# An adaLN-style layer on one core: GpSimd's low parts of x1 and x2 held back, the last tile's h turned earlier, sign's first slice in two transfers, 17 warm-ups for 19

## The reference

```python
base = einsum('btd,od->bto', x, W)
logits = einsum('btd,ed->bte', x, Wr) + 5.0 * one_hot(itok)[:, None, :]
topw, topi = top_k(logits, 2); weights = softmax(topw)
gates = sum(one_hot(topi, 8) * weights[..., None], axis=-2)
h = einsum('btd,erd->bter', x, A)
cond = base + 2.0 * einsum('bter,bte,eor->bto', h, gates, B)
out = x + einsum('bsi,io->bso', cond, sign) * softplus(scale)
```

## Time and profile before

| | us |
|---|---|
| median of 3 runs | 163.86 (163.75 to 163.94) |
| the profiled execution | 163.53 |
| its span (first to last instruction in the profile) | 161.3 |
| PE busy | 157.4 (98% of the span) |
| DVE busy | 110.0 (68%) |
| ACT busy | 63.6 (39%) |
| POOL busy | 52.2 (32%) |

### The profile page before, as it was taken

How to read it: one execution, slowest core, us unless ns; L and a number is a source line. 1 busy time by engine, 2 the same in 40 slices (tenths; PEclk the granted TensorE clock), 3 DMA queues, 4 the chain that set the end, 5 groups by cost and what they waited for, 6 DMA issues and landing times.

```text
span 161.3 us, 3653 instructions
## 1 busy us (share of the span) xinstructions
PE 157.4 (98%) x1046; PEld 151.8 (94%) x1046; DVE 110.0 (68%) x451; ACT 63.6 (39%) x178; POOL 52.2 (32%) x50
## 2 busy tenths in 40 slices
PE   8999999999999999999999999999999999999993
PEld 5887889899999999999999999999999999999992
DVE  5999999566666667666656666676666666666641
ACT  3645622244433334234344444433444343334432
POOL 2975554333330323333333333223132333333000
PEclk9999999999999999999999999999999999999999
DMA  5995332335545545344454545555555362223333
GB/s 178 376 150 131 107 107 74 89 76 150 147 142 148 142 104 180 106 135 123 126 142 136 139 142 146 143 146 145 144 146 145 86 189 81 62 62 87 130 130 130
DMA packets 45867, 21.47 MB, mean 133 GB/s; under 512 B 23680, under 2 KB 40864, under 8 KB 45856
## 3 DMA queue, kind: packets, MB, share of 16 engines
q1 hardware_dynamic: 30232, 13.58, 31.0%
q10 hardware_dynamic: 15624, 7.76, 16.6%
HBM read 11.03 MB, written 8.39 MB: 120 GB/s over the span
## 4 chain that ended last, share of the span: by engine, by line
PE 78%; DVE 11%; DMA 4%; issue 1%; SPq 1%; ACT 1%; ACTq 0%; DVEq 0%
PE pair L734 63%; PE pair L770 15%; DMA w_in<-in_L_cond_W 2%; DVE wide_lo L538 2%; DMA h_moved<-h_gated 2%; DVE m_full L532 2%; DVE w_lo L478 1%; DVE xt L488 1%; SPq L277 1%; DVE scale_spread L499 1%; DVE b_lo L543 1%; DVE second L616 1%; ACT w_hi L367 0%; ACT xt_hi L383 0%; DVE wide_lo L548 0%
## 5 line engine op out<-in xcount | busy, mean ns | idle before, releaser
L325 POOL TENSOR_TENSOR xt_lo<-xt,xt_hi 128x512 fp32r<-128x512 f32 x32 | 41.8, 1305 | 90.2 <-ACT xt_hi L383 90.2
L734 PE MATMUL pair<-wide_hi,xt_lo 128*128 128x392 f32 (+1 forms) x248 | 58.5, 311 | 0.0
L734 PE MATMUL pair<-wide_hi,xt_hi 128*128 128x392 f32 (+1 forms) x248 | 58.4, 311 | 0.0
L734 PE MATMUL pair<-wide_lo,xt_hi 128*128 128x392 f32 (+1 forms) x248 | 58.4, 312 | 0.0
L734 PEld LDWEIGHTS pair<-wide_hi,xt_hi 128*128 128x128 f32 x248 | 38.6, 188 | 0.4 <-issue 0.3
L734 PEld LDWEIGHTS pair<-wide_hi,xt_lo 128*128 128x128 f32 x248 | 38.6, 188 | 0.0
L734 PEld LDWEIGHTS pair<-wide_lo,xt_hi 128*128 128x128 f32 x248 | 38.5, 188 | 0.0
L447 ACT ACTIVATE y<-pair 128x256 f32<-128x256 f32 x31 | 11.9, 383 | 50.1 <-PE pair L770 50.1
L383 ACT ACTIVATE xt_hi<-xt 128x512 fp32r<-128x512 f32 x32 | 20.3, 633 | 9.7 <-DVE xt L488 7.9
L488 DVE STREAM_TRANSPOSE xt<-x_in 128x512 f32<-128x512 f32 x32 | 22.5, 703 | 0.0
L421 ACT ACTIVATE ht_hi<-ht 128x128 fp32r<-128x128 f32 x29 | 12.6, 433 | 24.1 <-DVE ht L580 24.1
(11 more groups left out here) (97 smaller groups left out, 142.5 us busy)
## 6 DMA issues: line engine op xcount, KB each, us to landing
out<-y SPq DMA_DIRECT2D x31, 256.0 KB, 2.3
x_in<-in_x ACTq DMA_DIRECT2D x104, 64.0 KB, 2.2
h_moved<-h_gated SPq DMA_DIRECT2D x116, 16.0 KB, 1.8
x_in<-in_x SPq DMA_DIRECT2D x24, 64.0 KB, 2.1
w_in<-in_L_cond_W SPq DMA_DIRECT2D x4, 256.0 KB, 4.4
sign_in<-in_L_ffn_sign ACTq DMA_DIRECT2D x3, 256.0 KB, 4.3
sign_in<-in_L_ffn_sign SPq DMA_DIRECT2D x1, 256.0 KB, 5.6
a_in<-in_L_cond_A SPq DMA_DIRECT2D x4, 64.0 KB, 4.0
```

What stands on the lines that cost most here:

```text
L325: nc.gpsimd.tensor_tensor(xt_lo[n][:, :, :].rearrange("p j (g b) -> p g j b", g=NQ), xt[n][:, :, :, :], xt_hi[n][:, :, :].bitcast(FP32).re ...
L734: last = nc.tensor.matmul(pair[n][bank][:, at0:at0 + hi - lo], l[:, k, :], w[:, k, lo:hi], start=(opens and k == 0 and l is xt_hi[n] and w ...
```

## The change

- POOL waits for `m_lo_made` 3 (DVE's last `low_m`) before `low_x` of tile 1, and, in step 0, for `gate_made` 1 (L623 of tile 0) before `low_x` of tile 2. PE starts tile 1 when its high part is there and waits for its low part only before the first matmul that reads it.
- In `finish` the transposition of h of tile 31 stands ahead of `lora` of tile 30; its parts get buffers of their own, `ht_hi_last` and `ht_lo_last`, and ACT's wait for `y_summed` is gone for it. `lora` of tile 31 on bank 0 stands ahead of the last three wide matmuls of bank 1.
- The first sign slice comes in two transfers of half the columns, 1 KB a row, with a semaphore for each; ACT thus issues four transfers for three. DVE's two casts wait for one each.
- 17 warm-ups instead of 19.

```diff
-    WARM_UPS = 19
+    WARM_UPS = 17
...
+            pool.wait_ge(m_lo_made, KC - 1)
             low_x(0, 1, 0)
 
             def step(q, r, s):
+                if s == 0:
+
+                    pool.wait_ge(gate_made, 1)
                 if has(s, LEAD):
                     low_x(q, r, LEAD)
...
-            for j in range(OC - 1):
+            act.dma_start(sign_in[:, 0, 0:HALF], sign_load[:, 0, 0:HALF]).then_inc(first_sign_loaded, 16)
+            act.dma_start(sign_in[:, 0, HALF:D], sign_load[:, 0, HALF:D]).then_inc(sign_loaded[0], 16)
+            for j in range(1, OC - 1):
                 act.dma_start(sign_in[:, j, :], sign_load[:, j, :]).then_inc(sign_loaded[j], 16)
...
-                    act.wait_ge(y_summed, late)
-                    nc.scalar.activation(ht_hi[:, :], p_ht[late][:, 0:P], ACT.Copy).then_inc(ht_hi_made, 1)
+                    if late == TILES - 1:
+                        nc.scalar.activation(ht_hi_last[:, :], p_ht[late][:, 0:P], ACT.Copy).then_inc(ht_hi_made, 1)
+                    else:
+                        act.wait_ge(y_summed, late)
+                        nc.scalar.activation(ht_hi[:, :], p_ht[late][:, 0:P], ACT.Copy).then_inc(ht_hi_made, 1)
...
             for j in range(EARLY):
+                dve.wait_ge(first_sign_loaded, 16)
+                nc.vector.tensor_copy(sign_hi[:, j, 0:HALF], sign_in[:, j, 0:HALF]).then_inc(first_sign_made, 1)
                 dve.wait_ge(sign_loaded[j], 16)
-                nc.vector.tensor_copy(sign_hi[:, j, 0:HALF], sign_in[:, j, 0:HALF]).then_inc(first_sign_made, 1)
...
                     for l, w in ((xt_hi[n], wide_hi), (xt_hi[n], wide_lo), (xt_lo[n], wide_hi)):
+                        if low_after_high and k == 0 and l is xt_lo[n]:
+                            pe.wait_ge(xt_lo_made, r + 1)
...
-                    pe.wait_ge(xt_lo_made, done + 1)
+                    if s == 1:
+                        pe.wait_ge(xt_hi_made, 2)
+                    else:
+                        pe.wait_ge(xt_lo_made, done + 1)
...
+                turn_h(s)
                 pe.wait_ge(ht_lo_made, s)
                 lora(before, (0, 1)).then_inc(y_summed, 1)
-                turn_h(s)
-                wide(r, second, (BANKS[1],))
+                wide(r, second[:1], (BANKS[1],))
                 pe.wait_ge(ht_lo_made, s + 1)
-                lora(r, (0,)).then_inc(last_summed, 1)
-                lora(r, (1,)).then_inc(y_summed, 1)
+                lora(r, (0,), ht_hi_last, ht_lo_last).then_inc(last_summed, 1)
+                wide(r, second[1:], (BANKS[1],))
+                lora(r, (1,), ht_hi_last, ht_lo_last).then_inc(y_summed, 1)
```

More of the change, by code:

```diff
@@ L119, in adaln_ffn_kernel @@
         ht_lo = sb("ht_lo", [ER, P], FP32R)
+        ht_hi_last = sb("ht_hi_last", [ER, P], FP32R)
+        ht_lo_last = sb("ht_lo_last", [ER, P], FP32R)
         y = [sb(f"y{n}", [P, D]) for n in range(RING)]
@@ L133, in adaln_ffn_kernel @@
         w_loaded = [sem(f"w_loaded{j}") for j in range(OC)]
+        first_sign_loaded = sem("first_sign_loaded")
         sign_loaded = [sem(f"sign_loaded{j}") for j in range(OC)]
@@ L570, in low_h @@
                                             ht_hi[:, :].bitcast(FP32).rearrange("p (b g) -> p g b", g=NQ),
+                                            ALU.subtract).then_inc(ht_lo_made, 1)
+                elif late == TILES - 1:
+                    nc.vector.tensor_tensor(ht_lo_last[:, :], p_ht[late][:, 0:P], ht_hi_last[:, :].bitcast(FP32),
                                             ALU.subtract).then_inc(ht_lo_made, 1)
@@ L723, in _, with wide @@
             last.then_inc(b2_summed, 1)
-            def wide(r, chunks, cols, opens=False, signals=False):
+            def wide(r, chunks, cols, opens=False, signals=False, low_after_high=False):
                 n = slot(r)
@@ L763, in first_tile, with lora @@
                                 last.then_inc((head_ready, wide_done)[bank], 1)
-            def lora(n, banks):
-                for l, w, stop in ((ht_hi, b2_hi, False), (ht_hi, b2_lo, False), (ht_lo, b2_hi, True)):
+            def lora(n, banks, h_hi=ht_hi, h_lo=ht_lo):
+                for l, w, stop in ((h_hi, b2_hi, False), (h_hi, b2_lo, False), (h_lo, b2_hi, True)):
                     for bank in banks:
@@ L789, in step @@
                         pe.wait_ge(b2_lo_made, 1)
-                    wide(r, range(KC // 2), BANKS, opens=True)
+                    wide(r, range(KC // 2), BANKS, opens=True, low_after_high=(s == 1))
                 if has(s, -LAG):
```

## The result

| | before | changed |
|---|---|---|
| median, us | 163.94 (20 runs, 163.34 to 164.86) | 163.21 (20 runs, 162.28 to 164.75) |
| ratio, with its 95% interval | | 0.9946 (0.9932 to 0.9961) |
| the profiled execution | 163.53 | 163.42 |
| its span | 161.3 | 161.6 |
| PE busy | 157.4 | 157.9 |

The change makes the kernel faster by 0.54%, 0.88 us (164 x 0.0054; 0.6 to 1.1 by the interval, and the two medians are 0.73 apart). I had forecast 1.14 us and 162.7. The two profiled executions, though, hardly differ, and the span of the changed one is longer. So the gain isn't to be read off the totals; it has to be found piece by piece. The three gains that I had forecast are there, and the start, which I had put at nothing, is a loss.

The account below looks back on a forecast made before the run. It took PE, busy 98% of the span, as the bound, with waits to remove. Gains 0.55 + 0.39 + 0.20 + 0 = 1.14 us took the profiled 163.53 to 162.39; plus 0.33 gave 162.7 us, range 162.3 to 163.2.

Parts of the forecast that it names:

- the terms' bounds: Low and high ends of all the forecast gains taken together, said to give 162.4 to 163.5 us.
- First hold: POOL waits for the third `low_m` before tile 1's low part; PE's first wait goes, -0.55 us, bounds -0.2 and -0.6.
- Second hold: POOL waits for tile 0's gate before tile 2's low part; PE's wait for tile 0's h goes, -0.39 us, bounds 0 and -0.39.
- With `gate_made` ahead of it POOL can't collide: Tile 0's gating: POOL's low part of tile 2 no longer overlaps L616, which took 1.10 us against 0.29.
- my 0.94: The two POOL waits' forecast gains together, 0.55 and 0.39 us.
- The end: In `finish`, tile 31's h is transposed before `lora` of tile 30; last matmul at 158.15 instead of 158.35, -0.20 us.
- The start: Split sign slice and two fewer warm-ups gain 0, since `w_lo` depends on neither; bounds -0.1 to +0.2 us.
- may land 0.3 us later than the whole did before it delays `w_lo`: At the start, the slack allowed to the second half of sign's first slice, 0.3 us.
- The sum: Whole kernel: gains of 0.55, 0.39, 0.20 and 0 make 1.14 us, for a time of 162.7 us.
- PE's last eight matmuls of tile 0 elsewhere than at 20.94: Sign that the forecast is wrong: these matmuls, ahead of tile 1, not beginning at 20.94 us.
- the warm pace later than 4.7: Sign that the forecast is wrong: PE's fast matmul pace at the start beginning later than 4.7 us.

Follow-up runs that it names:

- e1: Kernel before plus only both POOL waits and PE's later wait for tile 1's low part; 162.6 us, ratio 0.9908 to the kernel before.
- e8: Kernel before plus only POOL's wait ahead of tile 1's low part, with PE's later wait for it; 162.75 us, ratio 0.9928.
- e11: Kernel before plus POOL's wait ahead of tile 1's low part and the new `finish` order; one sign transfer, 19 warm-ups; 162.91 us, ratio 0.9929.
- e3: Kernel before plus only the split of sign's first slice into two column-half transfers, 19 warm-ups; 164.62 us, ratio 1.0035.
- e4: Changed kernel with sign's first slice in one transfer again, 17 warm-ups kept; 162.21 us, ratio 0.9885 to the kernel before.
- e5: Changed kernel with sign's first slice in one transfer and 19 warm-ups again; 162.56 us, ratio 0.9916 to the kernel before.
- e2: Kernel before plus only the new order in `finish` for tile 31's h, with its own buffers; 163.99 us, ratio 0.9999.
- e9: Kernel before plus only POOL's wait for tile 0's gate ahead of tile 2's low part; 163.24 us, ratio 0.9964.
- e6: Kernel before with sign's first slice in two transfers of 64 rows, 2 KB packets, both awaited before the first cast; 165.0 us, ratio 1.0078.
- e12: Changed kernel with sign's first slice in one transfer and 11 warm-ups instead of 17; 164.77 us, ratio 1.0060 to the kernel before.

## Why the prediction was right in its sum, and where it wasn't

The measured 163.21 lies at the very edge of 162.3 to 163.2, and the forecast direction is right. One sum in it is wrong: "the terms' bounds" add up to 162.5 to 163.9 (gains of 1.39 and of 0.2 - 0.2 = 0 under 163.86), not to 163.5. By its steps:

**First hold, -0.55: right.** Third `low_m` 0.65 for the forecast 0.67, POOL 1.30 for 1.29, start 0.08 behind the third, tile 1's low part in time although PE had 0.1 us to spare; no transposition hurt it. Tile 0 to tile 1 is 0.59 shorter in e1 and e8. The Trainium skill's rule of shared ports (SBUF — State Buffer, "SBUF: two separate sides") held: with POOL idle the same instruction takes 0.65 in place of 1.78.

**Second hold, -0.39: the size right in the trace (0.33), its owner in part wrong.** I took POOL's start for tile 2 (23.59) as fixed when I costed the holds one by one. But POOL is in order and idle behind the held instruction, and its next input was ready: both low parts then run back to back, end 1.0 to 1.2 us earlier than before, and hit the cast of `top_no` in place of `second`. With the first hold alone the collision costs 0.17 us (e8) or 0.68 us (e11) where it cost 0.8, and PE's loss shrinks to nothing or to 0.23. "With `gate_made` ahead of it POOL can't collide" is right: it is what removes the rest.

**Both together** are worth 0.92 us in the seams and 1.1 to 1.9 us by the time of e1, so my 0.94 is on the small side; the time of e8, 0.8 to 1.6, includes it.

**The end, -0.20: right, 0.17 in the trace;** too small for the time to show alone. From the start of `h_gated` to the last matmul I had worked out 2.55 (155.60 to 158.15); it is 2.59.

**The start, 0 with bounds -0.1 and +0.2: this step failed.** My argument was sound up to its last sentence. Nothing did hang on the warm-ups or on the first half, and I had written what the second half may cost: it "may land 0.3 us later than the whole did before it delays `w_lo`". I never put a number on how late it would land. It lands 1.0 later (5.09 for 4.11), 0.7 over the slack, and further transfers are late behind it. The trace of before had the number: of the three transfers of ACT's queue in the earlier trace rows the second, sign's second slice, was issued at 1.17 and landed at 5.46, 1.35 behind the first. The second half is issued at 1.18, in the very place of that slice. That was the bound to take: 1.35 less the slack of 0.3, a cost of up to 1.0 us rather than 0.2. The cost measured is 0.6 us alone (e3, 0.2 to 0.9) and 0.5 to 1.0 within the change (e4, e5).

**The sum.** By the measured parts: about -1.5 (e1), -0.2 (e2, trace) and +0.6 to +1.0 (e3, e4), -0.7 to -1.1, against -0.88 measured. My holds were too small by about as much as my start was too good. That the sum came out near is in part luck.

**What would show it wrong.** I had named two signs: PE's last eight matmuls of tile 0 elsewhere than at 20.94, and the warm pace later than 4.7. Both came (22.15; 5.6), and both were right as alarms: the first by the late data, the second by the pace. For the pace I had only one execution, with 4.6, and took it as the kernel's. The profiles of kernels with 17 or 19 warm-ups have it between 3.9 and 6.3, whichever number they have (19: 3.9, 3.9, 4.5, 4.5, 4.6, 4.6, 5.2, 5.8, 5.9, 6.3; 17: 3.9, 5.5, 5.6). The Trainium skill (TensorE: Matmul & The Clock Gate, "Part 1: The HAM clock gate") says the point varies from run to run; the traces agree, over a wider range than the 500 ns to either side that it gives, and the three close times before were no argument against it. Later than 4.7, a microsecond costs some 0.45 us at tile 0 (18.45 at 4.6 in e5, 19.20 at 6.3 in e1); earlier than 4.6 it gains nothing (18.48 at 3.9 in e9), since PE then waits for its first data. In kernels without the first hold a part of such a delay is hidden by the wait for the third `low_m`: in e6 tile 0's last eight matmuls begin 1.23 us later than before, tile 1 only 0.93. The changed kernel's executions scatter more than the others' (162.28 to 164.75), but that isn't for want of this cover: e8 has none either and lies within 162.07 to 163.20. What widens it is not shown.

**The best version** on record is the changed kernel with the slice in one transfer: 162.2 with 17 warm-ups (four executions), 162.6 with 19 (seven), against 163.2 and 163.9. Which number of warm-ups is better these don't tell.

## What to carry to other kernels

When a hold on one engine removes a collision, follow that engine's whole queue forward: what stood behind the held instruction moves too, and may do the next edit's work or undo it. When a transfer is split so that its first half may be used sooner, look up in the trace where the next transfer of that queue lands; the second half will land near there (here 0 to 0.4 us earlier), and the split pays only if its reader can wait so long. When an instruction stops being slow, look whether its neighbour has become slow instead. Before adding up gains against one profiled execution, ask which of its numbers vary between executions, as the start of the fast pace does here; and read it off the warm-ups too, not off the first interval behind a wait.

## What the runs showed of the hardware

- A half slice (128 KB) as the second transfer of ACT's queue is there at 5.09 to 5.22 us (e6, by rows: 5.50), hardly earlier than a whole slice (256 KB) in the same place (5.42 to 5.55 with 17 or 19 warm-ups); as the first transfer a half lands at 3.88 to 4.10 for 4.06 to 4.24. From 4 to 5 us the DMA engines are full (share 1.06, 399 GB/s before).
- The 256 KB in 256 packets of 1 KB land at 4.67, in 128 of 2 KB at 4.06 to 4.24.
- The granted clock stands at 1.00 in the first 19 us of the changed kernel and at 9 tenths throughout on both pages, while matmuls of 256 columns run 0.213 us apart at first. The pace, not that row, shows which level PE is at.
- After 11 warm-ups and a gap of 1.65 us the fast pace began only at 10.5 us; with 17 or 19 it began at 3.9 to 6.3. Once it had begun, it outlasted a gap: in e6 no matmul started between 4.27 and 6.04.
- `second`, an instruction of 128 x 8 with one tensor input, was blocked by a POOL subtraction (1.10 us for 0.29), and so was a cast of 128 x 2 (0.85 for 0.17, e11). A transposition of 128 x 512 was not (0.69 beside POOL's 1.31), nor was the MAX8 of 128 x 8 shortly before that cast (0.17 with and without POOL beside it, e11 and e5).

Left open: how much of the second transfer's microsecond is the queue and how much the full DMA engines; why SP's issues of B are drawn out in e12, which has no small packets; and up to 0.9 us lost in the middle of some executions, with and without the change, a part of it near 130 us. From the first `lora` to the transposition of tile 30's h it is 122.41 us in e4 and 123.36 in e1, which has this row:

```profile
129.79 0.54 PE L739 MATMUL pair<-wide_hi,xt_hi 128*128 128x392 f32 x2 [0.28 <-ACT y L452]
```

It may be a part of the scatter between runs. No run was made for it.
